# Rough-score rows moved by transfers of their own, begun by ScalarE, in a fused cross-attention and ternary FFN kernel

## The chip, the cores and the metric

The kernel runs on one core of a Trainium2 chip. The metric is the device time of one execution in microseconds (us), the median of several runs.

## What is computed

A gated cross-attention block with a ternary feed-forward network, in float32, for a batch of 128 with 128 rows of 256 values, 128 context rows of 192 values, and 16 heads of 16:

```
q, k, v = layernorm(x) @ Wq, ctx @ Wk, ctx @ Wv          # per batch, 16 heads of 16
attn    = softmax(mask(q k^T / 4)) v @ Wo
x       = x + tanh(g_xattn) * attn
h       = gelu(layernorm(x) @ ternary(W1)^T + b1)        # 1024 wide
out     = x + tanh(g_ffn) * (h @ ternary(W2)^T + b2)
```

## The kernel before, in words

Five instruction streams are written out by hand (TensorE, VectorE, ScalarE, GpSimd, SyncE), each in its own fixed order; they meet through semaphores. There are two stages: attention over 64 groups of two batches (until some 1060 us), then the feed-forward network over 32 steps of four batches. The change touches the attention stage alone.

A float32 product is made of 16-bit parts: q and k are each split in a high half (QH, KH: ScalarE's high_q and high_k, from PSUM) and a low half (QL, KL: VectorE's low_q and low_k, which read the high half). All four lie in qk16, of which there are two, by the parity of the group. Matmuls of a head need the head's 16 values on partitions, so transfers inside the on-chip memory move them from qk16 into qk_rows (also two, by parity): partitions 0 to 47 take QH/KH, QL/KH and QH/KL one below the other, partitions 48 and 49 the row maxima, and partitions 64 to 79 (RB) KH and QH once more. The exact scores (L418) read partitions 0 to 63; the rough scores (L381, from the high halves alone) read partitions 64 to 127.

The softmax needs the maximum of each row beforehand. So for each batch there are four units of four heads. A unit's rough scores are made, VectorE takes their maxima (take_max, L898), and after four units it rounds and splits them (round_max L906, low_max L913), TensorE transposes them (transpose_max, L396), ScalarE copies them (copy_maxT, L645), and SyncE moves them into qk_rows (move_max, L246). Only then can the exact scores of that batch be made, whose matmul subtracts the maxima. ScalarE takes the exponentials (L654), GpSimd splits them (L1059), and TensorE weighs v with them (L438 to L440).

A group on TensorE (pe_group) has eight slots, scores(g, b, u) for b = 0, 1 and u = 0 to 3. Each slot starts with four rough matmuls (L381) interleaved with four exact ones (L418). The rough ones are ahead: slot 0 makes (g, 1, 3); slots 1 to 4 make the four units of batch 0 of the next group g1; slots 5 to 7 make units 0 to 2 of its batch 1. Projections, transposes and weighings stand between. Slot 0 waits for the maxima of batch 0 (max_moved[0]) and slot 4 for those of batch 1. Slot 1, the first rough unit of a batch, waits in rough_free for all five transfers of its rows (qk_moved), and so does slot 5. transpose_max(g, 1) stands in slot 1, transpose_max(g1, 0) in slot 5.

SyncE's order in a group (sp_group) is: load the context rows of g + 3; move q and k rows of batch 1 of g + 1 (five transfers); move the maxima of batch 1 of g; move the q row of batch 0 of g + 2; in groups of parity 0 load x rows; move the maxima of batch 0 of g + 1; move the k rows of batch 0 of g + 2 (four transfers). Each transfer of rows waits for q_split or k_split, the low halves.

ScalarE's order in a group (act_group) is: exponentials 0 0, high_v, copy_ctxT, exponentials 0 1, copy_maxT of batch 1, high_q of g + 2, exponentials 0 2, copy_xT, exponentials 0 3, copy_attnT, exponentials 1 0, high_k of g + 2, exponentials 1 1, copy_maxT of batch 0 of g + 1, exponentials 1 2, apply_x, exponentials 1 3. VectorE's (dve_group) has the eight take_max, low_v, sum_weighed and normalise twice, low_q, low_attn, low_k and add_attention, and in groups of parity 1 seed_x, four steps of the next rows' layer norm.

Of the kernel before, what the change touches and what calls it, by code (L numbers as in the profile page):

```python
# [42 lines left out]
def bass_gated_cross_attention_ternary_ffn(  # L43
# [6 lines left out]
    HD = D // HEADS  # L50
# [16 lines left out]
    SR = HR + 2  # L67
    RB = 64
    RK = 64
    MOVES = 5  # L70
    MAX_UNIT = 64.0
    LAG = 2
    HBUF = 4
# [6 lines left out]
    with ExitStack() as top:  # L80
        def sem(name):
            return top.enter_context(nc.semaphore(name))
# [21 lines left out]
        qk_rows = [None] * 2  # L104
# [84 lines left out]
        q_made, q_high, q_split = sem("q_made"), sem("q_high"), sem("q_split")  # L189
        k_made, k_high, k_split = sem("k_made"), sem("k_high"), sem("k_split")  # L190
        v_made, v_high, v_split = sem("v_made"), sem("v_high"), sem("v_split")
        qk_moved = [sem(f"qk_moved{b}") for b in range(2)]
        weights_high, weights_split = sem("weights_high"), sem("weights_split")
        rough_scored, max_taken = sem("rough_scored"), sem("max_taken")
        max_rounded, max_split = sem("max_rounded"), sem("max_split")
# [26 lines left out]
        def rows_of(g, b, rows, i):  # L222
            return qk_rows[g.parity][rows, b, :, i].rearrange("d j m s -> d j (m s)")

        def move_q(sp, g, b, split, free):
            if free is not None:

                sp.wait_ge(scored, free)

            sp.wait_ge(q_split, split)  # L230
            sp.dma_start(rows_of(g, b, slice(0, HD), 0), qk16[g.parity][:, b, QH].rearrange("p m s -> p (m s)")
                         ).then_inc(qk_moved[b], 16)

        def move_k(sp, g, b, split):

            sp.wait_ge(k_split, split)
            sp.dma_start(rows_of(g, b, slice(0, HD), 1), qk16[g.parity][:, b, KH].rearrange("p m s -> p (m s)")  # L237
                         ).then_inc(qk_moved[b], 16)
            for r, i in ((HD, QL), (2 * HD, QH), (RB, KH)):
                sp.dma_start(qk_rows[g.parity][r:r + HD, b].rearrange("d j i m s -> d j (i m s)"),  # L240
                             qk16[g.parity][:, b, i:i + 2].rearrange("p i m s -> p (i m s)")).then_inc(qk_moved[b], 16)

        def move_max(sp, g, b, copied):

# [10 lines left out]
        def sp_group(sp, g, left):  # L255

            first = isinstance(g.half, int) and g.n == 0


            def held(value):  # L260
                return value if isinstance(value, int) else sp.snap(value)

            split1, split2 = held(g.n + 2), held(g.n + 3)
            scored_before = None if first else held(2 * UNITS * g.n)
            scored_b0 = held((g.n + 3) * (2 * UNITS) - 5 * UNITS)

            max_b1, max_b0 = held(g.batch(1) + 1), held(g.batch(0) + 3)
            x_past = held(g.half + 3) if g.parity == 0 else None
            if left >= 3:

                sp.wait_ge(ctx_transposed, split1)
                load_ctx(sp, g.after(3))
            if first:

                sp.wait_ge(rough_scored, UNITS + 1)
            if left >= 1:
                move_q(sp, g.after(1), 1, split1, scored_before)
                move_k(sp, g.after(1), 1, split1)
            move_max(sp, g, 1, max_b1)
            if left >= 2:  # L280
                move_q(sp, g.after(2), 0, split2, scored_b0)
            if g.parity == 0 and left >= 6:

                sp.wait_ge(ln_ready, x_past)
                load_x(sp, g.half + 3)
            if left >= 1:
                move_max(sp, g.after(1), 0, max_b0)
            if left >= 2:
                move_k(sp, g.after(2), 0, split2)

# [76 lines left out]
        def rough_free(pe, g, b, u):  # L369

            n = g.batch(b) * UNITS + u
            if not (isinstance(n, int) and n < 2):

                pe.wait_ge(max_taken, n - 1)
            if u == 0:

                pe.wait_ge(qk_moved[b], 16 * MOVES * (g.n + 1))

        def rough_head(pe, g, b, u, c):
            q, k = (qk_rows[g.parity][RB:RB + RK, b, (u * UH + c) // KD, i, c % KD, :] for i in (1, 0))  # L380
# [19 lines left out]
        def scores(pe, g, b, u, rough=None):  # L400


            n = g.batch(b) * UNITS + u
            if rough is not None:
                rough_free(pe, *rough)
            if u == 0:

                pe.wait_ge(max_moved[b], 16 * (g.n + 1))
            if not (isinstance(n, int) and n < 2):

                pe.wait_ge(exp_done, n - 1)
            for c in range(UH):
                if rough is not None:
                    made = rough_head(pe, *rough, c)
                    if c == UH - 1:
                        made.then_inc(rough_scored, 1)
                q, k = (qk_rows[g.parity][0:SK, b, (u * UH + c) // KD, i, c % KD, :] for i in (0, 1))
                last = pe.matmul(st_bank[u % 2][:, c * S:(c + 1) * S], k, q, start=True, stop=True)  # L418
            last.then_inc(scored, 1)
# [193 lines left out]
        def high_q(act, g):  # L613
            act.wait_ge(q_made, g.n + 1)
            if not (isinstance(g.half, int) and g.n < 2):

                for b in range(2):
                    act.wait_ge(qk_moved[b], 16 * MOVES * (g.n - 1))
            act.activation(halves_of(g, QH), pj_halves, ACT.Identity, bias=0.0,
                           scale=1.0 / WS).then_inc(q_high, 1)  # L620

# [76 lines left out]
        def act_group(act, g, left):  # L698
            first = isinstance(g.half, int) and g.n == 0
            g1, g2, g3 = g.after(1), g.after(2), g.after(3)  # L700
            before, g4 = g.after(-1), g.after(4)
            exponentials(act, g, 0, 0)
            if not first:
                high_v(act, g)
            if left >= 2:
                copy_ctxT(act, g2)
            exponentials(act, g, 0, 1)
            copy_maxT(act, g, 1)
            if left >= 2:
                high_q(act, g2)  # L710
            exponentials(act, g, 0, 2)
            if left >= 3:
                copy_xT(act, g3)
            exponentials(act, g, 0, 3)
            if not first:
                copy_attnT(act, before)
            exponentials(act, g, 1, 0)
            if left >= 2:
                high_k(act, g2)
            exponentials(act, g, 1, 1)  # L720
            if left >= 1:
                copy_maxT(act, g1, 0)
            exponentials(act, g, 1, 2)
            if left >= 4:
                apply_x(act, g4)
            exponentials(act, g, 1, 3)
            if left == 0:
                copy_attnT(act, g)
# [594 lines left out]
        def _(sp):  # L1323
# [17 lines left out]
            sp.wait_ge(pads_set, 4)  # L1341
            sp.wait_ge(k_rows_set, 2)
            for b in range(2):
                move_q(sp, Group(0, 0), b, 1, None)
                move_k(sp, Group(0, 0), b, 1)

            sp.wait_ge(ln_ready, 2)
            load_x(sp, 2)
# [1 line left out]
            sp.wait_ge(rough_scored, 1)  # L1350
            move_max(sp, Group(0, 0), 0, 1)
            sp.wait_ge(k_rows_set, 4)
            move_q(sp, Group(0, 1), 0, 2, None)
            move_k(sp, Group(0, 1), 0, 2)
            over_groups(sp, sp_group, 3)

            sp.wait_ge(scored, 2 * UNITS * (NG - 1))
# [108 lines left out]
```

## Time and profile before

| | |
|---|---|
| median of 3 runs | 1601.36 us (1598.82 to 1603.03) |
| the profiled execution | 1602.56 us, its span 1600.6 us |
| mean granted clock of TensorE | 0.971 |
| TensorE matmuls busy | 1351.8 us, 84% |
| VectorE busy | 1262.9 us, 79% |
| ScalarE busy | 975.4 us, 61% |
| GpSimd busy | 839.2 us, 52% |
| SyncE's DMA queue | 118.56 MB, 41.2% of 16 DMA engines |

The span is the time from the first to the last instruction. Engines' busy times overlap, so they don't add up. Idle time of an engine stands beside the instruction that came after it, with what released it. All rows further down are of this one execution; times in them count from the span's start.

### The profile page before, as it was taken

What the parts mean: (1) busy time and instruction counts of PE and PEld (TensorE: products, weight loads), DVE (VectorE), ACT (ScalarE), POOL (GpSimd) and SP (SyncE); (2) the same over time, 40 slices, a digit from 0 to 9 for tenths busy, and PEclk for the clock granted to TensorE, in tenths of its full rate; (3) what the DMA queues carried; (4) which work ended last, traced back from release to release, by engine and by line L of the source; (5) the groups of instructions that cost most, each with busy time, mean ns of one, the idle gap of its engine ahead of it and who ended that gap; (6) DMA issues with size and microseconds to landing.
All of it is one profiled execution on the core that took longest, in us unless ns stands there. A gap on an engine that the chain in (4) does not pass through costs nothing.

```text
span 1600.6 us, 52630 instructions
## 1 busy us (share of the span) xinstructions
PE 1351.8 (84%) x18085; PEld 1005.7 (63%) x18085; DVE 1262.9 (79%) x2998; ACT 975.4 (61%) x1683; POOL 839.2 (52%) x1233
## 2 busy tenths in 40 slices
PE   2788888888888888888888888868999999999998
PEld 2566666666666666666666666645666666666665
DVE  6687887778777877787788777778888888888886
ACT  3566666666666666666666667636555555555553
POOL 6477767777777777777777777631111111111110
PEclk9799999999999999999999999968999999999999
DMA  2655555565656565646565655420010101010101
GB/s 75 109 93 95 105 94 94 94 109 88 101 98 103 83 106 95 105 83 104 99 102 87 99 102 84 72 69 17 27 39 26 39 26 39 26 39 26 39 26 53
DMA packets 155729, 118.99 MB, mean 74 GB/s; under 512 B 22321, under 2 KB 155441, under 8 KB 155697
## 3 DMA queue, kind: packets, MB, share of 16 engines
q1 hardware_dynamic: 155696, 118.56, 41.2%
q8 instruction: 20, 0.33, 0.1%
q14 instruction: 13, 0.10, 0.0%
HBM read 32.53 MB, written 16.78 MB: 31 GB/s over the span
## 4 chain that ended last, share of the span: by engine, by line
PE 34%; DVE 21%; DMA 19%; issue 12%; SPq 8%; ACT 4%; DVEq 1%; POOL 0%; ACTq 0%; POOLq 0%
DMA qk_rows<-qk 13%; PE bank L1219 12%; DMA qk_rows<-smaxT 6%; DVE smax L898 6%; PE bank L1248 5%; PE bank L1249 5%; SPq L240 5%; PE bank L381 3%; DVE y L1206 2%; DVE stats L784 2%; PE bank L461 2%; DVE qk L855 2%; SPq L237 2%; PE bank L340 2%; DVE smax L906 2%
## 5 line engine op out<-in xcount | busy, mean ns | idle before, releaser
L1059 POOL TENSOR_TENSOR prob<-prob 128x512 f16<-128x512 f32 x512 | 533.9, 1043 | 258.7 <-ACT prob L654 250.8
L654 ACT ACTIVATE prob<-bank,masks 128x512 f32<-128x512 f32 x512 | 352.0, 688 | 277.4 <-PE bank L418 271.5
L898 DVE TENSOR_REDUCE smax<-bank 128x4 f32<-128x512 f32 x512 | 346.2, 682 | 149.5 <-PE bank L381 149.4
L381 PE MATMUL bank<-qk_rows 64*128 64x128 f16 x2048 | 206.2, 223 | 137.7 <-DMA qk_rows<-qk 70.3
L1230 ACT ACTIVATE hid<-bank,b_sb 128x512 f32<-128x512 f32 x256 | 175.9, 688 | 211.3 <-PE bank L1219 205.0
L1313 POOL TENSOR_TENSOR xres<-xres,b2g 128x1024 f32 (+1 forms) x32 | 75.3, 2354 | 430.6 <-ACT yln L1183 413.5
L1235 DVE TENSOR_TENSOR hidl<-hid 128x512 f16<-128x512 f32 x256 | 225.6, 881 | 80.6 <-ACT hid L1230 79.6
L1219 PE MATMUL bank<-y,w1T 128*128 128x512 f16 x1024 | 264.6, 381 | 28.8 <-DVE y L1206 27.6
L381 PEld LDWEIGHTS bank<-qk_rows 64*128 64x128 f16 x2048 | 117.7, 96 | 223.5 <-DMA qk_rows<-qk 86.0
L1248 PE MATMUL bank<-w2T,hid 128*128 128x256 f16 x1024 | 237.4, 273 | 0.6 <-ACT w2T L1159 0.6
L1249 PE MATMUL bank<-w2T,hidl 128*128 128x256 f16 x1024 | 237.3, 273 | 0.0
L438 PE MATMUL bank<-v,prob 128*128 128x32 f16 x2048 | 213.8, 181 | 1.6 <-POOL prob L1059 1.1
L440 PE MATMUL bank<-v,prob 128*128 128x32 f16 x2048 | 207.2, 178 | 0.0
L418 PE MATMUL bank<-qk_rows 64*128 64x128 f16 x2048 | 206.9, 223 | 0.2 <-DMA qk_rows<-smaxT 0.2
L439 PE MATMUL bank<-v,prob 128*128 128x32 f16 x2048 | 206.8, 177 | 0.0
L438 PEld LDWEIGHTS bank<-v,prob 128*128 128x128 bf16 x2048 | 165.2, 97 | 50.8 <-issue 2.5
L439 PEld LDWEIGHTS bank<-v,prob 128*128 128x128 bf16 x2048 | 168.5, 98 | 1.1
L440 PEld LDWEIGHTS bank<-v,prob 128*128 128x128 f16 x2048 | 165.9, 97 | 0.0
L1219 PEld LDWEIGHTS bank<-y,w1T 128*128 128x128 f16 x1024 | 97.9, 98 | 103.8 <-issue 34.8
L1248 PEld LDWEIGHTS bank<-w2T,hid 128*128 128x128 bf16 x1024 | 100.2, 98 | 39.6 <-ACT w2T L1159 1.1
L1249 PEld LDWEIGHTS bank<-w2T,hidl 128*128 128x128 f16 x1024 | 100.2, 98 | 38.6
L418 PEld LDWEIGHTS bank<-qk_rows 64*128 64x128 f16 x2048 | 116.7, 96 | 0.7 <-DMA qk_rows<-smaxT 0.4
(116 smaller groups left out, 2605.1 us busy)
## 6 DMA issues: line engine op xcount, KB each, us to landing
qk_rows<-qk SPq DMA_DIRECT2D x384, 128.0 KB, 4.0
xres<-in_x_dram SPq DMA_DIRECT2D x32, 512.0 KB, 3.5
qk_rows<-qk SPq DMA_DIRECT2D x256, 64.0 KB, 3.3
out_dram<-ystage SPq DMA_DIRECT2D x32, 512.0 KB, 3.0
ctx_sb<-in_ctx_dram SPq DMA_DIRECT2D x64, 192.0 KB, 4.0
qk_rows<-smaxT SPq DMA_DIRECT2D x128, 16.0 KB
w_raw<-in_L_ffn_W_dram SPq DMA_DIRECT2D x2, 1024.0 KB, 6.8
prob<-in_L_xattn_Wq_dram SPq DMA_DIRECT2D x1, 256.0 KB, 4.4
```

The lines of the kernel that those rows point to most:

```text
L381: return pe.matmul(sm_bank[u % 2][:, c * S:(c + 1) * S], q, k, start=True, stop=True)
L418: last = pe.matmul(st_bank[u % 2][:, c * S:(c + 1) * S], k, q, start=True, stop=True)
L438: pe.matmul(o, high, v_high, start=True, stop=False)
L439: pe.matmul(o, high, v_low, start=False, stop=False)
L440: last = pe.matmul(o, low, v_high, start=False, stop=True)
L654: act.activation(prob[u][:], st_bank[u % 2][:], ACT.Exp, bias=0.0, scale=masks[g.parity][:, 2 + b:3 + b]).then_inc(exp_done, 1)
L898: dve.tensor_reduce(smax[:, b, u * UH:(u + 1) * UH], sm_bank[u % 2][:].rearrange("p (h j) -> p h j", h=UH), AX.X, ALU.max).then_inc(max_ta ...
L1059: pool.tensor_tensor(prob[u][:].bitcast(F16)[:, 0::2], prob[u][:], prob[u][:].bitcast(BF16)[:, 1::2], ALU.subtract).then_inc(prob_split, 1)
L1219: last = pe.matmul(h_bank[f % 2][:], w1T[:, k, f * P:(f + 1) * P], y16[g.parity][:, part, k, :], start=(i == 0), stop=(i == 2 * KD - 1))
L1235: dve.tensor_tensor(hidl[f % HBUF][:], hid[f % HBUF][:], hid[f % HBUF][:].bitcast(BF16)[:, 1::2], ALU.subtract).then_inc(h_split, 1)
L1248: pe.matmul(o, high, w2T[:, f, :], start=(f == 0 and b % 2 == 0), stop=False, skip_group_check=True)
L1249: last = pe.matmul(o, hidl[f % HBUF][:, b * S:(b + 1) * S], w2T[:, f, :], start=False, stop=(f == FB - 1), skip_group_check=True)
```

## The change

The rows at partitions 64 to 79 get a transfer and semaphores of their own. move_rough waits for the high halves alone (q_high, k_high) and is issued by ScalarE, for both batches of g + 2, behind exponentials(g, 1, 1), one activation after high_k. The other four transfers of a batch are together in move_qk and stand behind move_max in SyncE's order: those of batch 1 behind the maxima of batch 1, those of batch 0 behind the maxima of batch 0. rough_free waits for the rough rows alone; the wait for the other rows moves to the first exact scores of a batch. The semaphores are now by parity and batch. The number of transfers and their bytes stay the same.

```diff
-    MOVES = 5
+    MOVES = 4
...
-        qk_moved = [sem(f"qk_moved{b}") for b in range(2)]
+        rough_moved = [[sem(f"rough_moved{p}{b}") for b in range(2)] for p in range(2)]
+        qk_moved = [[sem(f"qk_moved{p}{b}") for b in range(2)] for p in range(2)]
...
-        def move_q(sp, g, b, split, free):
+        def move_rough(queue, g, b, high):
+
+            queue.wait_ge(q_high, high)
+            queue.wait_ge(k_high, high)
+            queue.dma_start(qk_rows[g.parity][RB:RB + HD, b].rearrange("d j i m s -> d j (i m s)"),
+                         qk16[g.parity][:, b, KH:QH + 1].rearrange("p i m s -> p (i m s)")).then_inc(rough_moved[g.parity][b], 16)
+
+        def move_qk(sp, g, b, split, free):
             if free is not None:
 
                 sp.wait_ge(scored, free)
 
             sp.wait_ge(q_split, split)
-            sp.dma_start(rows_of(g, b, slice(0, HD), 0), qk16[g.parity][:, b, QH].rearrange("p m s -> p (m s)")
-                         ).then_inc(qk_moved[b], 16)
-
-        def move_k(sp, g, b, split):
-
             sp.wait_ge(k_split, split)
-            sp.dma_start(rows_of(g, b, slice(0, HD), 1), qk16[g.parity][:, b, KH].rearrange("p m s -> p (m s)")
-                         ).then_inc(qk_moved[b], 16)
-            for r, i in ((HD, QL), (2 * HD, QH), (RB, KH)):
+            for i, half in ((0, QH), (1, KH)):
+                sp.dma_start(rows_of(g, b, slice(0, HD), i), qk16[g.parity][:, b, half].rearrange("p m s -> p (m s)")
+                             ).then_inc(qk_moved[g.parity][b], 16)
+            for r, i in ((HD, QL), (2 * HD, QH)):
                 sp.dma_start(qk_rows[g.parity][r:r + HD, b].rearrange("d j i m s -> d j (i m s)"),
-                             qk16[g.parity][:, b, i:i + 2].rearrange("p i m s -> p (i m s)")).then_inc(qk_moved[b], 16)
+                             qk16[g.parity][:, b, i:i + 2].rearrange("p i m s -> p (i m s)")).then_inc(qk_moved[g.parity][b], 16)
...
+            move_max(sp, g, 1, max_b1)
             if left >= 1:
-                move_q(sp, g.after(1), 1, split1, scored_before)
-                move_k(sp, g.after(1), 1, split1)
-            move_max(sp, g, 1, max_b1)
-            if left >= 2:
-                move_q(sp, g.after(2), 0, split2, scored_b0)
+                move_qk(sp, g.after(1), 1, split1, scored_before)
...
             if left >= 1:
                 move_max(sp, g.after(1), 0, max_b0)
             if left >= 2:
-                move_k(sp, g.after(2), 0, split2)
+                move_qk(sp, g.after(2), 0, split2, scored_b0)
...
-                pe.wait_ge(qk_moved[b], 16 * MOVES * (g.n + 1))
+                pe.wait_ge(rough_moved[g.parity][b], 16 * (g.half + 1))
...
             if u == 0:
 
+                pe.wait_ge(qk_moved[g.parity][b], 16 * MOVES * (g.half + 1))
                 pe.wait_ge(max_moved[b], 16 * (g.n + 1))
...
                 for b in range(2):
-                    act.wait_ge(qk_moved[b], 16 * MOVES * (g.n - 1))
+                    act.wait_ge(rough_moved[g.parity][b], 16 * g.half)
+                    act.wait_ge(qk_moved[g.parity][b], 16 * MOVES * g.half)
...
             exponentials(act, g, 1, 1)
+            if left >= 2:
+                for b in range(2):
+                    move_rough(act, g2, b, g2.n + 1)
             if left >= 1:
                 copy_maxT(act, g1, 0)
```

The first groups' rows are moved by SyncE ahead of the loop, in the same two parts.

## Rows read from the trace of the kernel before

**Rows 1.** The page: shares of the chain that ended last; issues, KB, us to landing.
```profile
PE 34%; DVE 21%; DMA 19%; issue 12%; SPq 8%; ACT 4%; DVEq 1%; POOL 0%; ACTq 0%; POOLq 0%
DMA qk_rows<-qk 13%; PE bank L1219 12%; DMA qk_rows<-smaxT 6%; DVE smax L898 6%; PE bank L1248 5%; PE bank L1249 5%; SPq L240 5%; PE bank L381 3%; DVE y L1206 2%; DVE stats L784 2%; PE bank L461 2%; DVE qk L855 2%; SPq L237 2%; PE bank L340 2%; DVE smax L906 2%
...
qk_rows<-qk SPq DMA_DIRECT2D x384, 128.0 KB, 4.0
```

**Rows 2.** Stretch 516 to 832: length, busy us (instructions), clock, DMA share, GB/s.
```profile
516.00:832.00 316.00, 263.64 (x4580) 206.29 (x4578) 250.97 (x559) 214.93 (x379) 233.28 (x380) 0.98 0.59 97
```

**Rows 3.** List of waits, whole span: us in total, times, longest us.
```profile
PE bank L381 <- DMA qk_rows<-qk: 70.3, 51, 1.9
...
PE bank L381 <- DVE smax L898: 27.1, 27, 2.5
PE bank L381 <- DMA qk_rows<-smaxT: 26.8, 28, 1.1
```

**Rows 4.** Timeline of TensorE: start, us, what, [idle before <-releaser]; slots 0, 1, 4.
```profile
562.28 0.23 PE L381 MATMUL bank<-qk_rows 64*128 64x128 f16 x1
...
578.02 0.23 PE L381 MATMUL bank<-qk_rows 64*128 64x128 f16 x1
...
609.83 0.23 PE L381 MATMUL bank<-qk_rows 64*128 64x128 f16 x1
...
613.13 0.23 PE L381 MATMUL bank<-qk_rows 64*128 64x128 f16 x1 [1.38 <-DMA qk_rows<-qk]
...
618.62 0.21 PE L381 MATMUL bank<-qk_rows 64*128 64x128 f16 x1 [0.91 <-DVE smax L898]
...
621.34 0.22 PE L396 MATMUL bank<-ident,smax 128*128 128x128 f16 x1 [0.53 <-DVE smax L913]
...
625.69 0.23 PE L381 MATMUL bank<-qk_rows 64*128 64x128 f16 x1
```

**Rows 5.** Timeline of SyncE's DMA issues in the group from 609.83 (start, us).
```profile
607.78 1.88 SPq L240 DMA_DIRECT2D qk_rows<-qk  x3
...
614.97 0.55 SPq L246 DMA_DIRECT2D qk_rows<-smaxT  x1
...
621.95 0.55 SPq L246 DMA_DIRECT2D qk_rows<-smaxT  x1
```

**Rows 6.** Timeline of TensorE around the group of parity 0 from 595.25.
```profile
590.32 2.65 PE L461 MATMUL bank<-wo,attnT 128*128 128x256 f16 x12
...
595.25 0.23 PE L381 MATMUL bank<-qk_rows 64*128 64x128 f16 x1
...
597.22 0.23 PE L381 MATMUL bank<-qk_rows 64*128 64x128 f16 x1
...
599.87 0.62 PE L309 MATMUL bank<-ident,xln 128*128 128x128 f16 x8 [0.39 <-DVE attn L930]
...
602.96 0.22 PE L381 MATMUL bank<-qk_rows 64*128 64x128 f16 x1 [0.60 <-DMA qk_rows<-smaxT]
```

**Rows 7.** Three short stretches, columns as in rows 2 (the last two: DMA share, GB/s).
```profile
610.00:616.00 6.00, 4.62 (x97) 3.66 (x91) 4.47 (x9) 4.32 (x9) 3.13 (x4) 1.00 1.12 147
...
618.00:623.00 5.00, 3.80 (x65) 2.97 (x66) 4.90 (x17) 3.09 (x6) 3.55 (x8) 1.00 0.00 0
...
623.75:624.00 0.25, 0.25 (x9) 0.15 (x6) 0.25 (x1) 0.00 (x0) 0.25 (x1) 1.00 0.00 0
```

**Rows 8.** Timeline of ScalarE: exponentials(g, 1, 1), then copy_maxT of batch 0.
```profile
620.61 0.68 ACT L654 ACTIVATE prob<-bank,masks 128x512 f32<-128x512 f32 x1
621.67 0.26 ACT L645 COPY smaxT<-bank 64x128 f16<-64x128 f16 x1 [0.37 <-PE bank L396]
```

**Rows 9.** Source line L240: duration of an issue in ns, min/median/max.
```profile
L240 SPq DMA_DIRECT2D qk_rows<-qk x384: 552/599/1747, 37.2 to 1041.5; - x192
```

**Rows 10.** Timeline of VectorE: low_q and low_max in the group from 609.83.
```profile
615.47 0.69 DVE L849 SCALAR_TENSOR_TENSOR qk<-bank,qk 128x512 f16<-128x512 f32 x1 [0.59 <-ACT qk L619]
...
621.02 0.17 DVE L913 SCALAR_TENSOR_TENSOR smax<-smax 128x16 f16<-128x16 f32 x1
```

More of the change, by code:

```diff
@@ L1343, in _ @@
             for b in range(2):
-                move_q(sp, Group(0, 0), b, 1, None)
-                move_k(sp, Group(0, 0), b, 1)
+                move_rough(sp, Group(0, 0), b, 1)
+            for b in range(2):
+                move_qk(sp, Group(0, 0), b, 1, None)
             sp.wait_ge(ln_ready, 2)
@@ L1352, in _ @@
             sp.wait_ge(k_rows_set, 4)
-            move_q(sp, Group(0, 1), 0, 2, None)
-            move_k(sp, Group(0, 1), 0, 2)
+            for b in range(2):
+                move_rough(sp, Group(0, 1), b, 2)
+            move_qk(sp, Group(0, 1), 0, 2, None)
             over_groups(sp, sp_group, 3)
```

## The prediction

> **What bounds the kernel now.** I read the page's chain first, then the list of waits over the whole span, then one group of the attention stage step by step. The chain that ended last gives 13% of the span to the qk_rows<-qk transfers, 6% to qk_rows<-smaxT and 8% to SyncE's queue [rows 1], although every engine has idle time in the middle of that stage: of 316 us TensorE is busy 263.6, VectorE 251.0, GpSimd 233.3, ScalarE 214.9 [rows 2]. So the stage is held by a chain that runs through transfers, not by one engine. The list of waits names its ends at L381, the rough matmul with which each of the eight slots of a group begins: TensorE is idle there for 70.3 us until a qk transfer lands, 26.8 us until the maxima's transfer lands, 27.1 us put down to VectorE's maxima [rows 3]. Those three, 124 us, are the most that the change could give back.
>
> The slots tell which transfers these are. I call a group of parity 1 odd (VectorE also seeds the norms of later rows there) and one of parity 0 even. In the odd group that starts at 609.83, slot 1 starts at 613.13 after an idle 1.38, slot 4 at 618.62 after an idle 0.91, and the next group at 625.69 [rows 4]: 15.86 us in all. The even group from 562.28 to 578.02 takes 15.74 [rows 4]. A pair is 31.60. Slot 1 waits for batch 0's rows: SyncE issues the last three of their transfers from 607.78 to 609.66 [rows 5], because they stand behind move_max (L246) in its queue and behind k_split, and the last lands 3.5 us later. Slot 4 waits for batch 1's maxima: issued at 614.97 [rows 5], they are there 3.6 us later. The profile puts that wait down to VectorE, but in the even group of rows 6 the same slot is released by the smaxT transfer. For batch 0's maxima, issued at 621.95 [rows 5], the last bytes have moved by 623.75 [rows 7], 1.8 us after the issue. The difference is traffic: the DMA engines are full from 610 to 616 (share 1.12, 147 GB/s) and idle from 618 to 623 [rows 7], since SyncE sends both batches' ten transfers back to back and batch 1's maxima come behind them.
>
> **The change part by part.** *Taken away at slot 1:* the rough matmuls need only the rows RB and up, which need q_high and k_high but neither low half. Now ScalarE issues them, right behind exponentials(g, 1, 1), which it starts at 620.61 and ends at 621.29 [rows 8]. Two issues at SyncE's median 0.60 [rows 9] end by 622.5, and with 4.0 us to landing [rows 1] the second batch is there at 626.5, the first at 625.9. Slot 1 could start at 625.69 + 1.92 = 627.6 at the earliest (1.92 is 3.30 less the 1.38 idle [rows 4]). So the transfer is covered by 1.1 us and more, and the 1.38 goes. If the cover is lost, each further 1 us of issue or landing comes back as 1 us a group.
>
> *What is late next* has a natural experiment in the trace. At 590.32 the output projection L461 takes 2.65 us, and the transfers land meanwhile. The group after it starts at 595.25 and its slot 1 at 597.22, with no wait for qk: 1.97 instead of 3.30. It ends at 609.83, after 14.58 us, with 0.39 lost to normalise (slot 2's transposes) and 0.60 at slot 4 to smaxT [rows 6]. It is an even group.
>
> *Taken away at slot 4:* SyncE now sends batch 1's maxima first and its 384 KB of rows behind them, so the maxima should go through idle DMA engines, in 1.8 to 2.2 us rather than 3.6 (2.2 is my estimate, the 1.8 and some time to signal). That takes the 0.60 as well: an even group at 14.58 - 0.60 = 13.98.
>
> *An odd group* is then held by VectorE. Its low_q starts 2.34 after slot 1 (615.47 against 613.13) and low_max (L913) ends at 621.19, 5.72 later, with nothing but back to back work between them [rows 10]. The transposition of the maxima follows 0.15 later and the next group 4.35 after that (621.34 to 625.69 [rows 4]). Sum: 1.92 + 2.34 + 5.72 + 0.15 + 4.35 = 14.48. The pair: 13.98 + 14.48 = 28.46, which is 3.14 less than 31.60. Of the 64 groups I count 60 as of this kind, leaving two at each end (TensorE's matmuls wait for a qk transfer 51 times [rows 3], and where they don't, a stall before has taken its place, as at 590.32); 30 pairs give 94 us.
>
> *Added on ScalarE:* two DMA issues a group, 1.2 us. No DMA of ScalarE stands in the trace; the nearest rows are SyncE's, 0.55 at least and 1.75 at most [rows 9], and below that an issue could run wholly beside the activation in flight. I take 0.60, the median. Behind them in ScalarE's queue stand copy_maxT(g1, 0), exponentials (1, 2) and (1, 3) and apply_x. ScalarE has room: 214.9 of 316 us [rows 2]. The one with a deadline is copy_maxT (L645), now at 621.67 [rows 8]: SyncE waits for it, and slot 0 of the next group for the transfer. It can start at 621.29 + 1.2 = 622.5, 0.8 late; its transfer has 625.69 - 623.75 = 1.9 us to spare. But this transfer now meets the 256 KB of rough rows on the same DMA engines, 1.8 us of traffic at 147 GB/s. Were it to wait for all of it: 0.8 + 1.8 - 1.9 = 0.7 a group. Half of it or less leaves nothing. I take 0.1 a group, 6 us, and keep 0 to 42.
>
> *Moved on SyncE:* ten issues a group stay ten, eight of them on SyncE. The four for batch 1 start behind its maxima and the four for batch 0 behind batch 0's; load_x and load_ctx stand behind them. None is read before the scores of a later group, half a group away or more; the cover is 7 us and more, so I cost them at nothing. The added waits of ScalarE (q_high, k_high) are for its own earlier results and cost nothing; the wait for all four qk_moved counts ahead of high_q concerns transfers of a whole group before. TensorE's wait for the qk rows moves to scores and is long met. The FFN stage, from 1060 us on, is untouched.
>
> Sum: the profiled execution took 1602.6 us (span 1600.6); 1602.6 - 94 + 6 = 1514.6. The median of the runs shown is 1.2 lower: 1513.
>
> The Trainium skill (DMA: Bandwidth & Descriptors, section "Issuing engines are not separate DMA queues") speaks against the change: transfers begun by ScalarE and by SyncE run on the same 16 DMA engines and interleave, so a second issuing engine saves no more than issue time. By that rule batch 1's maxima might still meet traffic; what it would give is the second rival.
>
> **The rivals.** *Batch 0's maxima come late (slot 0 waits).* Two issues that block ScalarE and the rough rows' traffic ahead of the 16 KB: the 0.7 worked out above, 42 us in place of 6: 1549. For it: the two now start within 1 us of each other. Against: 1.9 us to spare, and the DMA engines are otherwise idle then.
>
> *Batch 1's maxima are no faster.* Bytes per group are the same, only spread. The even group keeps 14.58, 0.60 x 30 = 18 us lost: 1531. For it: batch 0's rows are now issued at the group's end and load_ctx behind them. Against: they are begun 7 us before these maxima.
>
> *More than forecast.* VectorE's low_q comes earlier with ScalarE's high_q, and all 124 us go: 1477.
>
> *Slower.* A DMA issue on ScalarE takes longer than on SyncE. copy_maxT is then late by 2i - 0.38 for an issue time i. A group saves 1.57 and has 1.9 to spare, so the change loses from i = 1.95 us without contention, and from about 1.05 us with its full 1.8. At i = 1.75, SyncE's longest [rows 9], and full contention: 3.1 + 1.8 - 1.9 - 1.6 = 1.4 a group, in 60 groups 84 us: 1685.
>
> *No change.* Something else ends slot 1's wait at the same time. The group of 14.58 us [rows 6] speaks against it.
>
> **How the numbers follow.** Forecast 0.47 (1490 to 1525), batch 1 no faster 0.14, batch 0 late 0.18, all waits gone 0.09, slower 0.08, no change 0.04. The range 1480 to 1560 takes in the first three and some of the fourth. A measurement of this kernel tells a change of 0.3% from none. Faster: 0.47 + 0.14 + 0.18 + 0.09 = 0.88; same 0.04; slower 0.08.
>
> **What would show it.** The profile after should have: no wait of L381 for a qk transfer; slot 1 some 1.95 us into the group; groups of 14.0 and 14.5 us in turn; the wait of the transposition (L396) for low_max grown in odd groups, 0.53 now; ScalarE issues of about 0.6 us; smaxT to slot 4 no longer a releaser. The prediction is wrong if slot 0 waits for smaxT, if ScalarE's issues are over 1 us, or if slot 2's wait for normalise grows well beyond 0.39.

## The result, and the profile after

The changed kernel takes 1591.04 us (median of 7 runs, 1583.69 to 1594.36) against 1603.03 us for the kernel before beside it. The ratio is 0.9922, 95% interval 0.9900 to 0.9945: faster by 0.8%, a small gain that is clear of the noise, where 5.6% was forecast (1513 us), and outside the range of 1480 to 1560. The profiled execution took 1594.36 us, its span 1592.3.

The page of the changed kernel: DMA queues (packets, MB, share), the chain's shares, and issues with KB and us to landing.

```profile
q1 hardware_dynamic: 137840, 102.30, 29.5%
q10 hardware_dynamic: 17856, 16.26, 5.4%
...
PE 47%; DVE 18%; DMA 14%; issue 12%; ACT 4%; ACTq 4%; DVEq 1%; POOL 0%; POOLq 0%
DMA qk_rows<-smaxT 14%; PE bank L1225 12%; PE bank L382 6%; PE bank L1255 5%; PE bank L1254 5%; DVE smax L904 5%; PE bank L353 4%; ACTq L230 3%; DVE y L1212 2%; PE bank L463 2%; PE bank L310 2%; PE bank L440 2%; PE bank L341 2%; DVE v L895 2%; PE bank L451 2%
...
xres<-in_x_dram SPq DMA_DIRECT2D x32, 512.0 KB, 4.5
...
qk_rows<-qk ACTq DMA_DIRECT2D x124, 128.0 KB, 3.7
```

The rough rows have a queue of their own (q10). The qk_rows<-qk transfers are gone from the chain, where they had 13% [rows 1], and the maxima's transfer has gone from 6% to 14%. The list of waits says the same: L382, the rough matmul (L381 before), waits no more for qk rows, but 70.2 us for the maxima, where it was 26.8 [rows 3].

```profile
PE bank L382 <- DMA qk_rows<-smaxT: 70.2, 49, 4.0
```

TensorE's timeline gives the groups. The rows of L382 here are slot 0 of four groups in a row (the even ones start at 433.28 and 463.59), the other two are waits inside the odd group.

```profile
433.28 0.22 PE L382 MATMUL bank<-qk_rows 64*128 64x128 f16 x1 [0.23 <-DMA qk_rows<-smaxT]
...
449.28 0.23 PE L382 MATMUL bank<-qk_rows 64*128 64x128 f16 x1 [2.00 <-DMA qk_rows<-smaxT]
...
453.80 0.62 PE L310 MATMUL bank<-ident,xln 128*128 128x128 f16 x8 [0.41 <-DVE attn L936]
...
458.96 0.22 PE L397 MATMUL bank<-ident,smax 128*128 128x128 f16 x1 [0.55 <-DVE smax L919]
...
463.59 0.23 PE L382 MATMUL bank<-qk_rows 64*128 64x128 f16 x1 [0.21 <-DMA qk_rows<-smaxT]
...
479.85 0.29 PE L382 MATMUL bank<-qk_rows 64*128 64x128 f16 x1 [2.25 <-DMA qk_rows<-smaxT]
```

The odd group from 449.28 takes 14.31 us (15.86 before [rows 4]): both of its old waits, 1.38 at slot 1 and 0.91 at slot 4, are gone. The even groups, from 433.28 and 463.59, take 16.00 and 16.26 us, more than the 15.74 of before. Their eighth slot ends in a wait of some 2 us at slot 0 of the next group, for the maxima of batch 0. These are issued and landed so (SyncE's timeline; ScalarE's; then the chain in order of time: start, us, what):

```profile
441.92 0.39 SPq L253 DMA_DIRECT2D xres<-in_x_dram  x1
444.16 0.56 SPq L250 DMA_DIRECT2D qk_rows<-smaxT  x1
```

```profile
442.30 0.68 ACT L657 ACTIVATE prob<-bank,masks 128x512 f32<-128x512 f32 x1
442.49 1.21 ACTq L230 DMA_DIRECT2D qk_rows<-qk  x2
443.87 0.26 ACT L648 COPY smaxT<-bank 64x128 f16<-64x128 f16 x1 [0.89 <-PE bank L397]
```

```profile
444.16 5.07 DMA qk_rows<-smaxT
...
460.08 3.39 DMA qk_rows<-smaxT
```

In the even group load_x (512 KB) and the rough rows (256 KB) are both begun in the 2.3 us ahead of the maxima, and these take 5.07 us from the issue to the landing, the moment at which the waiting engine is told. In the odd group, without load_x, it is 3.39 us, and slot 0 waits 0.2. Before, slot 0 started 3.74 us after the issue and waited for nothing (621.95 to 625.69 [rows 5, 4]), so the landing took no longer than that.

Two moments must be kept apart here: when the bytes are through, and when the landing is told. The maxima are the only packets of 256 bytes in the trace, 64 of them. In the odd group the last one ends at 462.20, 2.1 us after the issue, and the landing is 1.3 us later; in the even group it ends at 447.59, 3.4 us after the issue, and the landing is 1.6 us later. Before, the bytes were through in 1.7 to 1.8 us.

There is a second piece. Slot 0 could have started at 449.28 - 2.00 = 447.28, only 3.12 us after SyncE's issue, against 3.73 before. The maxima are issued 0.6 us late: ScalarE's two issues stand ahead of copy_maxT, which starts after an idle 0.89, where it was 0.18 and 0.37 before (even group at 605.81; odd group in rows 8). Of the 2.0 us of the wait, 0.6 are this delay and some 1.4 the longer landing.

While slot 0 waits, the DMA engines are full and TensorE has little to do, as the last two of these stretches show; in the first load_x and the rough rows are in flight (columns as in rows 2):

```profile
444.00:445.00 1.00, 1.00 (x18) 0.91 (x16) 0.97 (x3) 1.00 (x3) 1.00 (x3) 1.00 1.06 365
...
447.00:448.00 1.00, 0.28 (x3) 0.00 (x0) 0.00 (x0) 0.00 (x0) 0.43 (x1) 1.00 1.17 139
448.00:449.00 1.00, 0.00 (x0) 0.00 (x0) 0.00 (x0) 0.00 (x0) 0.00 (x0) 1.00 1.14 139
```

The third piece is TensorE's clock. 12 of the 30 odd groups between 70 and 1020 us take 16.3 to 18.6 us instead of 14.3, among them the one from 513.67. Its timeline, and its stretches:

```profile
513.67 0.29 PE L382 MATMUL bank<-qk_rows 64*128 64x128 f16 x1 [2.31 <-DMA qk_rows<-smaxT]
...
525.64 0.22 PE L397 MATMUL bank<-ident,smax 128*128 128x128 f16 x1 [1.56 <-DVE smax L919]
```

```profile
514.00:517.00 3.00, 3.00 (x38) 2.14 (x36) 2.61 (x5) 2.32 (x4) 1.81 (x2) 0.52 0.36 51
517.00:520.00 3.00, 3.00 (x71) 2.37 (x67) 2.15 (x6) 2.30 (x5) 1.47 (x3) 1.00 0.01 1
...
527.00:531.00 4.00, 4.00 (x50) 3.07 (x48) 2.73 (x6) 1.68 (x4) 3.36 (x7) 0.57 0.37 92
```

After an idle 2.31 us the granted clock is about half (1.2 in place of 2.4 GHz) in the stretch that follows, and once more after the 1.56 us wait of slot 5. The group takes 17.6 us. The clock's record bears it out for the stage: exactly these 12 groups have stretches at half clock, 75 us of them together, and none of the other 48 groups has any. Why these 12 is open: the first of them waits 4.0 us at slot 0 and the others 1.8 to 2.4, but most of the 18 others wait 1.8 to 2.4 us as well. The kernel before has such drops too, in 9 groups; the L461 of 2.65 us in rows 6 is one, as this stretch of its trace shows:

```profile
590.50:591.00 0.50, 0.50 (x4) 0.35 (x3) 0.50 (x2) 0.47 (x1) 0.50 (x1) 0.50 0.00 0
```

There they cost next to nothing, because the transfers landed meanwhile and the next group was shorter by as much: the group with this drop takes 17.23 us and the next 14.57, together 31.80 where a pair takes 31.72 on average. Now an odd group has little wait left that could absorb them.

So of the stage between 70 and 1020 us, 60 groups before and after, the sum is 951.7 us before (31.72 a pair) and 949.0 after (16.03 for an even and 15.60 for an odd group on average, 31.63 a pair). What slots 1 and 4 gave was taken back at slot 0 and by the clock. Of the 8.3 us by which the span is shorter, 5.8 come from the last two full groups, behind 1020 us (33.8 us before, 28.0 after).

### The profile page after: what moved, and what is told of

Its sections match the earlier page's. It is cut to its first block, busy times and chain, and to the rows that moved or that the text cites. A ratio compares the mean times of both kernels' runs of the same rounds, so it can differ in the third digit from the quotient of the medians.

```text
span 1592.3 us, 52891 instructions
## 1 busy us (share of the span) xinstructions
PE 1368.8 (86%) x18085; PEld 1014.7 (64%) x18085; DVE 1271.2 (80%) x2998; ACT 970.9 (61%) x1683; POOL 839.4 (53%) x1233
## 3 DMA queue, kind: packets, MB, share of 16 engines
q10 hardware_dynamic: 17856, 16.26, 5.4%
## 4 chain that ended last, share of the span: by engine, by line
PE 47%; DVE 18%; DMA 14%; issue 12%; ACT 4%; ACTq 4%; DVEq 1%; POOL 0%; POOLq 0%
DMA qk_rows<-smaxT 14%; PE bank L1225 12%; PE bank L382 6%; PE bank L1255 5%; PE bank L1254 5%; DVE smax L904 5%; PE bank L353 4%; ACTq L230 3%; DVE y L1212 2%; PE bank L463 2%; PE bank L310 2%; PE bank L440 2%; PE bank L341 2%; DVE v L895 2%; PE bank L451 2%
## 5 line engine op out<-in xcount | busy, mean ns | idle before, releaser
L382 PE MATMUL bank<-qk_rows 64*128 64x128 f16 x2048 | 210.0, 226 | 78.0 <-DMA qk_rows<-smaxT 70.2
L382 PEld LDWEIGHTS bank<-qk_rows 64*128 64x128 f16 x2048 | 118.8, 97 | 163.0 <-DMA qk_rows<-smaxT 69.0
L420 PE MATMUL bank<-qk_rows 64*128 64x128 f16 x2048 | 210.6, 226 | 0.3 <-issue 0.3
L341 PE MATMUL bank<-xT,wq 128*128 128x256 bf16 (+1 forms) x768 | 116.1, 293 | 6.1 <-DVE wo L871 6.1
```

The source lines that it names most:

```text
L382: return pe.matmul(sm_bank[u % 2][:, c * S:(c + 1) * S], q, k, start=True, stop=True)
```

## The experiments

Theory T: the DMA traffic begun just ahead of batch 0's 16 KB of maxima (the rough rows, and in even groups load_x with them) delays them, and slot 0 waits. Rival I: ScalarE's two issues hold up copy_maxT, and that is why slot 0 waits. Rival O: SyncE's new order is what made them late. Each kernel here starts from the changed one unless it says otherwise; before was run beside each, at 1600 to 1603 us.

**load_x behind the maxima** (x_behind):

```diff
-            if g.parity == 0 and left >= 6:
-                sp.wait_ge(ln_ready, x_past)
-                load_x(sp, g.half + 3)
             if left >= 1:
                 move_max(sp, g.after(1), 0, max_b0)
             if left >= 2:
                 move_qk(sp, g.after(2), 0, split2, scored_b0)
+            if g.parity == 0 and left >= 6:
+                sp.wait_ge(ln_ready, x_past)
+                load_x(sp, g.half + 3)
```

> The changed kernel with load_x (512 KB, in groups of parity 0) issued behind move_max and move_qk of batch 0 instead of ahead of them; nothing else differs. Traffic theory: in the changed kernel's groups of parity 0, slot 0 of the next group waits some 2.2 us (16.2 us a group against 14.33 in groups of parity 1) because batch 0's maxima (16 KB) share the DMA engines with load_x's 512 KB and the rough rows' 256 KB: 5.1 us from issue to landing. Without load_x ahead the landing takes about 3.4 us as in the other parity, both parities take 14.3 to 14.5 us, and the groups of 17.5 us at half clock get rarer: 1505 to 1525 us. Rival, ScalarE's issue time delays copy_maxT: that delay stays, the time stays within 5 us of the changed kernel's 1591.

Measured: 1506.51 us, ratio 0.9422 (0.9397 to 0.9448). Both parities take 14.3 us. TensorE's slot 0 after an even and after an odd group, and one landing from the chain:

```profile
444.16 0.23 PE L382 MATMUL bank<-qk_rows 64*128 64x128 f16 x1 [0.31 <-DMA qk_rows<-smaxT]
...
458.49 0.22 PE L382 MATMUL bank<-qk_rows 64*128 64x128 f16 x1 [0.23 <-DMA qk_rows<-smaxT]
```

```profile
454.96 3.40 DMA qk_rows<-smaxT
```

ScalarE's issues are where they were, and so is their 0.6 us of delay. T holds and I is refuted as the main cause. The delay is where the 0.2 to 0.3 us that are left come from: a landing of 3.4 to 3.5 us would fit into the 3.73 of before. One transfer's place is worth some 80 us (ratios 0.9422 and 0.9922). The mean granted clock of its profiled run is 0.985 against the changed kernel's 0.959: with the idle time the drops went as well.

**The rough rows one step behind copy_maxT** (rough_behind):

```diff
-            if left >= 2:
-                for b in range(2):
-                    move_rough(act, g2, b, g2.n + 1)
             if left >= 1:
                 copy_maxT(act, g1, 0)
+            if left >= 2:
+                for b in range(2):
+                    move_rough(act, g2, b, g2.n + 1)
```

> The changed kernel with ScalarE's two issues of the rough rows behind copy_maxT(g1, 0) instead of ahead of it; nothing else differs. Traffic theory: the maxima's transfer is issued some 0.5 us earlier and the rough rows' bytes come behind it; it lands in 2.2 to 3 us in both parities, slot 0 waits no more, groups take 13.9 to 14.4 us: 1490 to 1520 us. Rival, issue time alone is what delayed the maxima: only 0.5 us a group comes back, 1560 us. A third way: the rough rows now land too late for slot 1, whose wait would be back: 1570 us or more.

Measured: 1568.9 us, ratio 0.9777 (0.9739 to 0.9815), a miss for T as I had put it. ScalarE's issue came at 462.78, still 0.2 us ahead of SyncE's, which has to be told first that the copy is done. The chain gives the maxima's way in an odd and an even group:

```profile
462.78 1.21 ACTq L230 DMA_DIRECT2D qk_rows<-qk  x2
```

```profile
462.99 4.45 DMA qk_rows<-smaxT
...
477.77 5.37 DMA qk_rows<-smaxT
```

Here nothing holds up copy_maxT: slot 0 could start 3.80 us after the maxima's issue. It waits all the same, for the landing. Side by side is worse than 1.7 us ahead, as in the changed kernel (4.45 against 3.39 in odd groups). That left two readings: a second queue's packets are served beside the maxima whenever they come, or what was issued first counts.

**SyncE issues the rough rows, behind the maxima** (rough_sp; load_x stays ahead):

```diff
             if left >= 1:
                 move_max(sp, g.after(1), 0, max_b0)
             if left >= 2:
+                for b in range(2):
+                    move_rough(sp, g.after(2), b, split2)
                 move_qk(sp, g.after(2), 0, split2, scored_b0)
...
-            if left >= 2:
-                for b in range(2):
-                    move_rough(act, g2, b, g2.n + 1)
```

> The changed kernel, but SyncE issues both rough transfers, right behind move_max of batch 0 and ahead of move_qk of batch 0; ScalarE issues none, load_x stays ahead of the maxima. The run rough_behind, with ScalarE issuing at the same moment as SyncE, left slot 0 waiting 0.85 us in groups of parity 1 and 1 to 2.5 us in those of parity 0. If the engine's queue decides (packets of two queues take turns, packets of one queue go in order), the maxima go ahead of the rough rows here and slot 0 waits no more in parity 1 and little in parity 0: groups of 14.0 to 14.5 us, 1490 to 1515 us. If only the bytes near the maxima in time decide, it is like rough_behind: 1560 to 1575 us. If the rough rows now come too late for slot 1, its wait is back.

Measured: 1480.94 us, ratio 0.9238 (0.9222 to 0.9253). Groups of 13.68 and 14.12 us. SyncE's queue in an even group, and slot 0 of the next, which waits for nothing:

```profile
515.03 0.40 SPq L253 DMA_DIRECT2D xres<-in_x_dram  x1
516.60 0.57 SPq L250 DMA_DIRECT2D qk_rows<-smaxT  x1
517.34 1.21 SPq L230 DMA_DIRECT2D qk_rows<-qk  x2
```

```profile
520.33 0.23 PE L384 MATMUL bank<-qk_rows 64*128 64x128 f16 x1
```

load_x 1.6 us ahead, alone, does no harm: the maxima are there within 520.33 - 516.60 = 3.7 us. It takes the rough rows with it. ScalarE issues nothing here, so that this run takes away the traffic and the delay of copy_maxT at once.

**ScalarE issues them, but later** (act_behind_apply): the three lines of move_rough stand behind apply_x(act, g4) in act_group instead of ahead of copy_maxT.

> The changed kernel with ScalarE's two issues moved two steps back, behind apply_x, so that they come some 0.5 to 1 us after SyncE has issued batch 0's maxima: the same moment at which rough_sp (1481 us, slot 0 without a wait) issues them, but on ScalarE's queue. load_x stays ahead. If the queue decides (the rough rows' packets of a second queue are served beside the maxima, though issued later), slot 0 waits as in rough_behind: 1545 to 1575 us. If only the order in time decides, it is like rough_sp: 1480 to 1500 us, and what hurt in the change was that the rough rows went ahead of the maxima.

Measured: 1476.72 us, ratio 0.9226 (0.9192 to 0.9260), the best of all and not to be told from rough_sp. The gain thus needs no issue on ScalarE, only rough rows that are begun early enough for slot 1 and behind the maxima. SyncE, ScalarE and TensorE in turn:

```profile
513.29 0.56 SPq L250 DMA_DIRECT2D qk_rows<-smaxT  x1
```

```profile
513.85 0.55 ACTq L230 DMA_DIRECT2D qk_rows<-qk  x1
```

```profile
517.03 0.23 PE L382 MATMUL bank<-qk_rows 64*128 64x128 f16 x1
```

0.56 us behind the maxima on the other queue, and slot 0 does not wait. The order in time decides, not the queue; my reading of rough_sp by its single queue falls.

**Issue time without the traffic** (tiny_issues; from rough_sp, two transfers of 64 bytes issued by ScalarE ahead of copy_maxT, with a wait for the pair of the group before):

```diff
+            if left >= 2:
+                if not first:
+                    act.wait_ge(tiny_moved, 32 * g.n)
+                for b in range(2):
+                    act.dma_start(tiny[:, b], ones[0:1, 0:16]).then_inc(tiny_moved, 16)
             if left >= 1:
                 copy_maxT(act, g1, 0)
```

> rough_sp (SyncE issues the rough rows), with two DMA issues of 64 bytes each added on ScalarE where the change has its two, ahead of copy_maxT: ScalarE's issue time without the traffic. In rough_sp the maxima land some 1.5 us ahead of slot 0. If issue time were the cause of slot 0's wait in the change, it would appear here: 1520 us or more. By the traffic theory copy_maxT is 0.3 to 0.6 us later, the slack covers it, and the time stays at 1481 to 1490 us.

Measured: 1479.59 us, ratio 0.9248 (0.9231 to 0.9264), as rough_sp. The issues and the copy, and slot 0 without a wait:

```profile
511.48 1.16 ACTq L732 DMA_DIRECT2D tiny<-ones  x2
512.83 0.26 ACT L652 COPY smaxT<-bank 64x128 f16<-64x128 f16 x1 [0.70 <-PE bank L401]
```

```profile
516.35 0.23 PE L386 MATMUL bank<-qk_rows 64*128 64x128 f16 x1
```

So 1.2 us of issuing on ScalarE costs nothing here, and rival I is not enough by itself. It still does something: copy_maxT starts after an idle 0.70 where rough_sp has 0.21, and slot 0 is left 3.25 us from the maxima's issue instead of 3.73. The landing fits into both. Where it does not fit, the delay is paid in full, as in the changed kernel. The medians over the groups of the stage show both pieces (us; "left" is from the issue of batch 0's maxima to the moment at which slot 0 could start but for them, "even" and "odd" the group in which they are issued):

| run | left, even / odd | slot 0 waits, even / odd |
|---|---|---|
| before | 3.73 / 3.73 | 0 / 0 |
| changed kernel | 3.12 / 3.30 | 2.16 / 0.21 |
| x_behind | 3.12 / 3.30 | 0.33 / 0.21 |
| rough_behind | 3.80 / 3.80 | 1.14 / 0.76 |
| rough_sp, act_behind_apply | 3.73 / 3.73 | 0 / 0 |
| tiny_issues | 3.25 / 3.44 | 0 / 0 |
| b1_late | 3.77 / 3.73 | 0.61 / 0 |

**Half the bytes ahead** (b1_late): ScalarE issues batch 0's rough rows alone where the change has both; batch 1's follow exponentials(g, 1, 3). load_x stays ahead.

> The changed kernel, but only batch 0's rough rows (128 KB) are issued ahead of copy_maxT; batch 1's follow exponentials(g, 1, 3). load_x stays ahead. Traffic theory: half the bytes of the second queue and one issue less ahead of the maxima: slot 0 waits 0 instead of 0.3 us in groups of parity 1 and about 1 instead of 2.2 us in those of parity 0: 1530 to 1560 us. If the amount does not matter but only that a second queue is busy: within 10 us of 1591. If load_x alone is at fault, too: near 1591.

Measured: 1496.07 us, ratio 0.9350 (0.9321 to 0.9379), better than expected. Behind odd groups slot 0 no longer waits, behind even ones it waits 0 to 1.3 us, 0.6 in the middle:

```profile
496.87 0.23 PE L382 MATMUL bank<-qk_rows 64*128 64x128 f16 x1 [1.01 <-DMA qk_rows<-smaxT]
```

The amount matters. But the run takes away more than these bytes: with only one issue ahead of it copy_maxT is on time again (3.77 us left in the table, not 3.12). Of the 1.5 us that slot 0 waits less behind even groups, 0.65 are this, and 0.9 a shorter landing.

**The halves of the change.** First ScalarE's part alone, with SyncE's old order (act_alone): move_qk is taken apart again, batch 1's four transfers stand ahead of move_max(g, 1), and batch 0's q row ahead of load_x.

> One half of the change alone: ScalarE moves the rough rows where the change has them, and SyncE moves the other four transfers of each batch in its old order (batch 1's ahead of the maxima of batch 1, batch 0's q row early). Traffic theory: slot 1 is free, batch 1's maxima stay late at slot 4 (3.6 us from issue to landing), and batch 0's maxima still meet load_x and the rough rows: 16.2 us and 14.5 us for the two parities, 1590 to 1605 us. Rival, the reordering on SyncE is what made slot 0 late: without it groups take 14.6 us and the time is 1530 us.

Measured: 1581.07 us, ratio 0.9863 (0.9839 to 0.9887). TensorE's slot 0 after an even and an odd group:

```profile
452.35 0.23 PE L402 MATMUL bank<-qk_rows 64*128 64x128 f16 x1 [2.19 <-DMA qk_rows<-smaxT]
...
467.03 0.22 PE L402 MATMUL bank<-qk_rows 64*128 64x128 f16 x1 [0.58 <-DMA qk_rows<-smaxT]
```

Slot 0 waits in the old order too: rival O is out. The new order even costs 10 us here (1591.04 against 1581.07; the intervals of the ratios do not meet); part of it may be the clock, at half for 75 us of the stage in the changed kernel and for 37 in act_alone. Second, SyncE's order alone, with all five transfers of a batch on SyncE and the rough rows last (sp_order_alone).

> The other half alone: all five transfers of a batch stay together on SyncE, the rough rows last, but in the change's order (batch 1's behind the maxima of batch 1, batch 0's behind the maxima of batch 0). ScalarE issues nothing. Expected: slot 4 no longer waits for batch 1's maxima (0.6 to 0.9 us less), slot 1 waits as before or 0.6 us longer since the q row is issued behind the maxima too; groups of 15.3 to 16 us: 1575 to 1605 us. If slot 0 waited here as well, the reordering and not the rough rows would be its cause.

Measured: 1744.6 us, ratio 1.0893 (1.0875 to 1.0912), a clear miss. It is slot 5, the first rough unit of batch 1, that waits most, some 3 us a group, and slot 1 only 0.5. SyncE issues batch 1's rough rows, last of the five, at 466.07, and slot 5 starts 4.1 us later. The profile names no releaser there, but such a transfer takes 4.0 us to land [rows 1]. Half clock follows in all 60 groups.

```profile
466.07 0.55 SPq L230 DMA_DIRECT2D qk_rows<-qk  x1
```

```profile
470.15 0.21 PE L384 MATMUL bank<-qk_rows 64*128 64x128 f16 x1 [2.93 <-issue]
```

The new order is only possible because the rough rows don't stand last in it; rough_sp shows that they may stand on SyncE's queue in another place. And is it worth anything? act_alone suggested that it isn't, since slot 4 did not wait there. The last run asks again where slot 0 no longer hides it (apply_old_order: act_behind_apply with SyncE's old order).

> act_behind_apply (ScalarE issues the rough rows behind apply_x, 1477 us) with SyncE's old order: batch 1's four transfers ahead of the maxima of batch 1, batch 0's q row ahead of load_x. It shows what the reordering on SyncE, the other half of the change, is worth once slot 0 no longer waits. act_alone showed slot 4 without a wait in the old order (1.87 us to slot 4, as in the changed kernel). So: nothing to 10 us, 1475 to 1490 us. If batch 1's maxima were late behind 384 KB of rows as in the kernel before: slot 4 waits 0.5 us or more a group, 1510 us or more.

Measured: 1573.22 us, ratio 0.9821 (0.9799 to 0.9844), 96 us more than act_behind_apply. Slot 4 waits again:

```profile
496.61 0.22 PE L402 MATMUL bank<-qk_rows 64*128 64x128 f16 x1 [1.69 <-DMA qk_rows<-smaxT]
```

In act_alone the wait at slot 0 had given batch 1's rows the time to move on: the bytes of batch 1's maxima were through 1.7 to 1.9 us after their issue, here in 2.7 and 3.5. With slot 0 free the wait comes back at slot 4. The two waits hide each other. Of the 96 us a part is the clock's: 31 of the 60 groups run at half clock for a stretch behind slot 4.

**Three more with load_x behind**, meant to take away x_behind's last 0.3 us:

> As rough_sp, with load_x behind move_qk of batch 0 as in x_behind. Queue-order theory: batch 0's maxima have the DMA engines to themselves, as in the kernel before (slot 0 without wait, against 0.3 to 0.4 us in x_behind): 14.0 to 14.1 us a group, 1485 to 1500 us. If ScalarE's issues ahead of copy_maxT cost nothing and the traffic is the same for both, it equals x_behind's 1506.

> As x_behind, but ScalarE issues only batch 0's rough rows ahead of copy_maxT; batch 1's follow exponentials(g, 1, 3), three slots later. Half of the 256 KB and one of two issues ahead of the maxima are gone: their landing goes from 3.4 to some 2.8 us and slot 0 waits 0 instead of 0.3 to 0.4: 14.0 us a group, 1485 to 1500 us. If these 0.3 us come from something else than issue time and traffic: 1506.

> As act_alone (ScalarE moves the rough rows, SyncE keeps its old order), with load_x behind the last rows of batch 0. The run act_alone showed slot 4 without a wait in the old order as well. So the reordering on SyncE should be worth little: slot 0 waits 0.6 us as in act_alone's groups of parity 1, in both parities: 14.7 us a group, 1520 to 1530 us against 1506 for x_behind. If the order matters once load_x is away, slot 4 waits again: 1540 us or more.

Measured: 1559.54 (0.9728, 0.9712 to 0.9745), 1559.97 (0.9725, 0.9704 to 0.9746) and 1585.34 us (0.9887, 0.9870 to 0.9903). The first two missed; the third came out in its last case, slot 4 waiting again. All three lose in the odd group, 16 to 18 us against 14.3, and in all three the clock is at half in part of the odd groups (in 28 of the 30 in the first two, in 19 in the third). In x_behind_sp load_x is issued 1.2 us into the odd group instead of 0.1, and batch 1's maxima meet it and the rows ahead of it:

```profile
569.30 0.21 PE L384 MATMUL bank<-qk_rows 64*128 64x128 f16 x1 [1.56 <-DMA qk_rows<-smaxT]
```

In x_behind_b1_late the first step of seed_x waits for the late load. I read the loss from that: it moves VectorE's chain, slot 4 waits 0.4, and a drop of the clock follows in 28 of the 30 odd groups. No run takes the steps apart:

```profile
534.24 1.41 DVE L791 BATCH_NORM_STATS2 stats<-xres 128x6 f32 x4 [0.41 <-DMA xres<-in_x_dram]
```

load_x behind the maxima is thus a place with little room (1.2 us into the odd group was too late, 0.3 too in x_behind_b1_late, whose groups are shorter, and 0.1 was not), and x_behind happened to fit in it. Moving the rough rows is the sturdier cure.

## Why the prediction was wrong

- *Slot 1.* Right: no wait for qk rows; slot 1 begins 1.87 us into the group, where 1.92 was worked out. The landing (3.7, median) and the issues (0.55 and 0.56) are a little under the 4.0 and 0.60 that were taken.
- *Slot 4.* Right: no wait, in either parity, but for 0.2 to 0.4 in odd groups that run at half clock. The bytes of batch 1's maxima are through 1.7 us after the issue, where it was 2.5 to 2.6. apply_old_order shows that the new order is what does it.
- *The odd group.* 14.48 was worked out along VectorE, 14.31 measured at full clock, of which 0.21 is slot 0's wait for the maxima. The path itself is 14.10: from low_q to the end of low_max it takes 5.23 (453.58 to 458.81) and not 5.72. The wait of slot 2 for normalise is 0.41 (0.39 was named). The wait of the transposition for low_max was to grow from 0.53; it is 0.55.
- *The even group* is where it failed: 13.98 against 16.03 on average, and 2.05 of these are the wait at slot 0, which the prediction had named as its first sign of being wrong. Over 30 groups that is some 62 us. The step is the term for batch 0's maxima, "0.8 + 1.8 - 1.9 = 0.7" with full contention, of which the sum took "0.1 a group". The 0.8, for the late copy, measured 0.6. The 1.9 "to spare" was counted from the moment at which the bytes were through (623.75) and left out the time until the landing is told, 1.3 us and more in the changed kernel. By that, my estimate of the landing before is 1.7 + 1.3 = 3.0 us of the 3.73 there were: 0.7 to spare. The 1.8 of contention counted the rough rows' traffic and left out load_x, which the prediction only says to stand behind the rows; in even groups it stands ahead of move_max in both kernels. In the profile before it did no harm there (issued at 603.89, the maxima at 606.09, and slot 0 at 609.83 waited for neither), and rough_sp shows that alone it still doesn't. With the rough rows added the landing is 5.3 us in the middle and slot 0 waits 1.8 to 2.4. The mechanism was named as the first rival, at 1549 with a chance of 0.18; its place was right, its size was a third of what even groups have. For odd groups the forecast 0.1 was near the 0.2 measured, but by luck: too much to spare and too much contention made up for each other.
- *The clock* was left out of the sum. 12 odd groups of 17.5 instead of 14.5 us cost 37 us, about the half of the 75 us that were granted at half clock. 61.5 and 36.7, less the 3 us by which the other 18 odd groups were shorter than worked out, are 95 us; the stage took 949.0 us against the 30 x 28.46 = 853.8 of the sum, 95 more.
- *ScalarE's issue time*, of which the slower rival was made: an issue took 0.55 us and not the 1.05 or more that this rival needs. Alone it costs nothing (tiny_issues), beside the traffic it is 0.6 of the 2.2 us of slot 0's wait behind even groups, and all of the 0.2 behind odd ones.
- *The Trainium skill's rule* (DMA: Bandwidth & Descriptors, section "Issuing engines are not separate DMA queues"), that transfers from both engines run on the same 16 DMA engines and interleave: the runs agree. rough_sp and act_behind_apply, on one queue and on two, are within each other's intervals. I had tied it to the wrong transfer, batch 1's maxima; it was batch 0's that met the traffic.

With the rough rows begun 0.6 us behind the maxima, still by ScalarE, the change gives what was forecast for it and more: 1476.72 us. That all of the 124 us of waits gone had been put at 1477 is a match of the sum; no run tests the reason given there, an earlier low_q.

## What to carry to other kernels

For a small transfer with a deadline, list what is issued in the 2 to 3 us ahead of it on every queue, its own and the others', with bytes; a large transfer without a deadline belongs behind it, and being behind by half a microsecond was enough here. Count its slack to the landing, not to the end of its bytes. When a wait is removed, look at each wait that it used to hide, and try the parts of a change again once the new bottleneck is gone: the same reordering cost 10 us beside one stall and was worth 96 us without it. A slack that absorbs drops of the clock is part of the time of the kernel before; a chain without slack pays for them.

## What the runs showed of the hardware

- A DMA issue on ScalarE is begun while the activation ahead of it still runs (442.49 in an activation from 442.30 to 442.98) and takes 0.55 us, as on SyncE. Two of them delay the copy behind them by 0.3 to 0.6 us (slot 0 is left 3.12 to 3.44 us, not 3.73); tiny_issues, where the landing fits into that, is no slower for it.
- The maxima's 16 KB, from the issue to the end of the bytes and to the landing: 1.7 to 1.8 us and at most 3.7 with nothing beside them [rows 5, 7]; 2.1 and 3.4 with 256 KB of rows begun 1.7 us ahead; 2.4 and 4.5 with these begun 0.2 us ahead; 3.4 and 5.1 with 512 KB of load_x ahead as well. The landing comes 1.3 to 2.1 us behind the last byte, latest where rows are moving beside it.
- Full DMA engines do not have one rate: 147 GB/s from 610 to 616 before [rows 7], 139 while slot 0 waits in the changed kernel, and 365 from 444 to 445 there, with load_x and the rough rows in flight. Why rows begun beside the maxima cost more than rows begun ahead of them, and why load_x costs nothing without them, no run here settles.
- With some 2 us of idleness at slot 0 the granted clock fell to half in 12 of 30 groups (0.52 from 514 to 517, after an idle 2.31); with the wait gone, in x_behind, in 1 group of the 60. That the idleness is the cause is my reading; most of the 18 groups without a drop had the same wait. The mean granted clock was 0.971 before, 0.959 in the changed kernel, 0.985 in x_behind.
